# Reordering the score, copy and transpose steps of a first-layer attention pipeline

## The reference

```
xn  = layernorm(x)
q,k,v = Q xn, K xn, V xn              # 16 heads of 64
p   = softmax(causal(q k^T / d_query))
x1  = x + (W (p v) scaled) + ffn(xn)  # ffn: shared unit + 32 experts, top 6, silu(gate) * up
```

## Time and profile before

| | us |
|---|---|
| median of 3 runs (lowest, highest) | 1194.99 (1194.1, 1196.14) |
| the profiled execution | 1194.1 |
| its span | 1192.2 |
| PE busy | 1171.3 (98%) |
| DVE busy | 983.1 (82%) |
| ACT busy | 810.1 (68%) |
| POOL busy | 407.2 (34%) |

### The profile page before, as it was taken

The page is one execution under the profiler, slowest core; times in us unless marked ns, Lnnn a source line. Parts: engine busy times, 40 slices in busy tenths (PEclk is TensorE's granted clock), DMA queues, the critical chain, the costliest instruction groups (busy, mean ns, idle before and its releaser), DMA issues.

```text
span 1192.2 us, 23821 instructions
## 1 busy us (share of the span) xinstructions
PE 1171.3 (98%) x8908; PEld 897.7 (75%) x8908; DVE 983.1 (82%) x1918; ACT 810.1 (68%) x2182; POOL 407.2 (34%) x364
## 2 busy tenths in 40 slices
PE   8999999999999999999999999999999999999998
PEld 6777687767777777677767776777777777767866
DVE  5988588979897989698969886989797878988886
ACT  6885577557755775677567756775577668767775
POOL 1317420640064007300630073006400768526820
PEclk9999999999999999999999999999999999999999
DMA  7004200310041003100410041004100410000000
GB/s 261 2 30 147 88 1 30 125 62 2 30 125 63 1 30 130 58 1 30 134 54 2 30 137 51 2 30 140 47 2 30 151 37 2 10 10 19 1 11 28
DMA packets 44292, 63.93 MB, mean 54 GB/s; under 512 B 8144, under 2 KB 18384, under 8 KB 43920
## 3 DMA queue, kind: packets, MB, share of 16 engines
q1 hardware_dynamic: 44176, 62.39, 16.2%
HBM read 59.48 MB, written 2.88 MB: 52 GB/s over the span
## 4 chain that ended last, share of the span: by engine, by line
PE 82%; DVE 9%; ACT 5%; issue 2%; DMA 1%; SPq 1%; POOL 0%; ACTq 0%; DVEq 0%; POOLq 0%
PE psum L1507 13%; PE psum L1529 12%; PE psum L1454 12%; PE psum L65 10%; PE psum L67 9%; PE psum L66 9%; PE psum L1564 4%; DVE mneg L1146 3%; ACT probs L766 3%; PE psum L1464 2%; PE psum L1756 1%; PE psum L1533 1%; PE psum L1819 1%; PE psum L1406 1%; DVE sg L1196 1%
## 5 line engine op out<-in xcount | busy, mean ns | idle before, releaser
L766 ACT ACTIVATE probs<-psum,mneg 128x256 f32<-128x256 f32 (+3 forms) x528 | 253.0, 495 | 166.5 <-DVE mneg L1146 165.5
L1146 DVE TENSOR_REDUCE mneg<-psum 128x2 f32<-128x1024 f32 (+2 forms) x320 | 245.2, 819 | 46.5 <-PE psum L1464 44.1
L1137 DVE COPY pt<-psum 128x512 f32<-128x512 f32 x320 | 205.7, 682 | 47.4 <-PE psum L1507 45.5
L1507 PE MATMUL psum<-ident,probs 128*128 128x128 f32 x1600 | 210.7, 276 | 3.8 <-DVE pt L1137 1.6
L1507 PEld LDWEIGHTS psum<-ident,probs 128*128 128x128 f32 x1600 | 178.2, 141 | 31.8 <-ACT probs L766 12.2
L573 POOL TENSOR_TENSOR qk_lo<-sg,qk_hi 128x512 fp32r<-128x512 f32 x64 | 92.4, 1450 | 159.0 <-ACT qk_hi L820 159.0
L1529 PE MATMUL psum<-pt,v_all 128*64 128x384 f32 (+5 forms) x1088 | 142.6, 412 | 0.0
L537 POOL TENSOR_TENSOR rstd<-var,mhalf 128x4 f32<-128x4 f32 x7 | 7.1, 1010 | 383.4 <-DVE var L1032 383.4
L1454 PE MATMUL psum<-qk_hi 64*128 64x512 f32 (+7 forms) x640 | 114.2, 353 | 5.4 <-DVE qk_lo L1131 3.6
L1529 PEld LDWEIGHTS psum<-pt,v_all 128*64 128x64 f32 (+1 forms) x1088 | 69.7, 135 | 63.0 <-issue 50.6
L65 PE MATMUL psum<-xt_hi,gu_hi 128*128 128x512 f32 x272 | 111.1, 409 | 0.7 <-DVE sg L1186 0.6
(11 more groups left out here) (276 smaller groups left out, 2506.0 us busy)
## 6 DMA issues: line engine op xcount, KB each, us to landing
crow<-weights SPq DMA_DIRECT2D x256, 128.0 KB, 2.9
rrow<-sums SPq DMA_DIRECT2D x128, 128.0 KB, 3.0
gu_raw<-in_gu SPq DMA_DIRECT2D x1, 2176.0 KB, 11.4
x_all<-in_x SPq DMA_DIRECT2D x8, 256.0 KB, 5.5
out_rows<-x_all SPq DMA_DIRECT2D x7, 256.0 KB, 2.3
down_raw<-in_down SPq DMA_DIRECT2D x1, 1088.0 KB, 13.5
wqkv_raw<-in_wqkv SPq DMA_DIRECT2D x1, 896.0 KB, 6.7
wqkv_raw<-in_wqkv SPq DMA_DIRECT2D x1, 512.0 KB, 4.8
```

The lines of the kernel that those rows point to most:

```text
L766: last = act.activation(probs[:, h * HALF + PROB[t]:h * HALF + PROB[t] + w], bank[score_bank(rnd, c) + h][:, o:o + w], ACT.Exp, bias=mneg[ ...
L1137: dve.tensor_copy(turned_rows(rnd)[:, s % 2, :, 3 - s // 2, :], turn_bank(rnd, s).rearrange("p (j q) -> p j q", q=P)).then_inc(pt_ready, 1)
L1146: last = dve.tensor_reduce(mneg_h[:, :, t], psum[:, b:b + 2, o:o + P * (t + 1)], AX, ALU.max, negate=True)
L1507: last = nc.tensor.transpose(turn_bank(rnd, s)[:, i * P:(i + 1) * P], probs[:, v:v + P], ident[:, :])
```

## The change

- TensorE, in each slot but the last of an item: chunk 2 of round n now comes before chunk 0 of round n+1. The wait for the low part of k of round n+1 stands before chunk 2; the wait for the exponentials stands before chunk 0.
- VectorE, in slots 0 to 5: the copy of T3 now stands before `rest_k`.
- TensorE, slots 6 and 7 and unit 0: `turn_acc` moves from slot 6 to slot 7, behind T0, T1 and T2, which now stand together; it writes bank 6 for all items but the last, and so waits for `copy_y`. T3 and T4 stand alone between the halves of unit 0. The wait on `x1_ready` moves from T0 of slot 7 to the weighted values behind unit 1. VectorE's `add_rows` moves from slot 6 to slot 7.
- ScalarE: the table load with its tiny activation goes from slot 7; a load stands now where the first Silu needs it.

```diff
--- before.py
+++ after.py
@@ -245,7 +245,7 @@
 
         def rows_bank(b):
 
-            return bank[7]
+            return bank[6] if b < B - 1 else bank[7]
 
         WEIGHTS_BANK = bank[6]
 
@@ -858,8 +858,6 @@
                         round_k(n + 2)
                     if p == PAIRS - 2:
                         copy_combt(b)
-                    if p == PAIRS - 1:
-                        load_table(ACT.Silu)
                     take_tile1(n)
                     if b == 0 and p >= PAIRS - len(DOWN_PIECES):
 
@@ -1216,11 +1214,12 @@
                     invert_sums(n)
                     if p < PAIRS - 2:
                         rest_q(n + 2, SCALE0)
-                        rest_k(n + 2)
                     if p < PAIRS - 1:
                         take_turned(n, [3])
-                    if p == PAIRS - 2 and b:
+                    elif b:
                         add_rows(b - 1)
+                    if p < PAIRS - 2:
+                        rest_k(n + 2)
                 n = b * PAIRS + PAIRS - 1
                 for u in range(UNITS):
                     if u == 0:
@@ -1622,14 +1621,15 @@
                     pe.wait_ge(pt_ready, (n - 1) * (TURNS - 1) + 3)
                 score_masks(n, 1, True)
                 score_products(n, 1, n % 2, ROWS0, True).then_inc(scored, 1)
-                if p < PAIRS - 1:
-                    pe.wait_ge(qk_lo_ready, (n + 1) * 2 + 2)
-                    pe.wait_ge(exp_done, exp_count(n, 0))
-                    score_products(n + 1, 0, (n + 1) % 2, ROWS0)
                 if p:
                     pe.wait_ge(pt_ready, n * (TURNS - 1))
                     pe.wait_ge(pt4_ready, n)
+                if p < PAIRS - 1:
+                    pe.wait_ge(qk_lo_ready, (n + 1) * 2 + 2)
                 score_products(n, 2, n % 2, ROWS0)
+                if p < PAIRS - 1:
+                    pe.wait_ge(exp_done, exp_count(n, 0))
+                    score_products(n + 1, 0, (n + 1) % 2, ROWS0)
                 score_masks(n, 2).then_inc(scored, 1)
                 if p < PAIRS - 1:
                     score_masks(n + 1, 0).then_inc(scored, 1)
@@ -1647,11 +1647,6 @@
                     weigh_pair(n - 1)
                 elif b:
                     project_out(b - 1, 3).then_inc(acc_done, 1)
-                if p == PAIRS - 1:
-                    if b:
-                        pe.wait_ge(x1_ready, b)
-                    turn_step0(n, 0)
-                    return
                 for s in range(3):
                     turn_step0(n, s)
                 if p < PAIRS - 2:
@@ -1662,14 +1657,15 @@
                     project_qk(n + 2, [0])
                     pe.wait_ge(pt_ready, n * (TURNS - 1) + 1)
                     project_qk(n + 2, [1])
-                else:
+                elif p == PAIRS - 2:
                     pe.wait_ge(y_ready, n)
                     turn_weights(b)
-                    if b:
-                        pe.wait_ge(pt_ready, n * (TURNS - 1) + 1)
-                        turn_acc(b - 1)
-                turn_step0(n, 3)
-                turn_step0(n, 4)
+                elif b:
+                    pe.wait_ge(y_ready, n)
+                    turn_acc(b - 1)
+                if p < PAIRS - 1:
+                    turn_step0(n, 3)
+                    turn_step0(n, 4)
 
             def first_head(b):
 
@@ -1692,13 +1688,13 @@
             def units(b):
                 n = (b + 1) * PAIRS - 1
                 half_unit(b, 0, 0)
-                turn_step0(n, 1)
-                turn_step0(n, 2)
+                turn_step0(n, 3)
                 half_unit(b, 0, 1).then_inc(gu_done, 1)
-                turn_step0(n, 3)
                 turn_step0(n, 4)
                 pe.wait_ge(pt_ready, n * (TURNS - 1) + 3)
                 project_unit(b, 1)
+                if b:
+                    pe.wait_ge(x1_ready, b)
                 pe.wait_ge(y_ready, n)
                 weigh_pair(n)
                 turn_sums0(b)
```

## The result

The changed kernel takes 1216.24 us (median of 4 runs, 1215.68 to 1217.07) where the kernel before took 1194.55 beside it (4 runs, 1192.04 to 1196.14). The ratio is 1.0184, with a 95% interval of 1.0165 to 1.0203: slower, by 1.7 us more than the forecast of 1214.5, and inside its range. The profiled execution took 1215.57 us, its span 1213.8, so 21.6 us more than before. ScalarE's lines keep their numbers in the changed kernel, VectorE's are 2 less, TensorE's 1 less.

The account below looks back on a forecast made before the run. TensorE was taken as the bound, busy 1171.3 of 1192.2 us. Terms 8.8 - 0.1 + 8.4 + 2.4 = 19.5 us on the profiled 1194.1 gave 1213.6; with the median 0.9 higher, 1214.5 us, range 1202 to 1222.

Parts of the forecast that it names:

- Regular slots: Slots 1 to 5 of eight items: TensorE waits for low k, 0.22 us a slot, 8.8 us in all.
- without any feedback: Regular slots, if a longer slot gave ScalarE and VectorE no earlier start: 0.36 us a slot, the upper bound.
- Slot 6: Without turn_acc seven items save 0.27 but the wait for k adds 0.22: 7.56 us long, -0.1 us in all.
- Slot 7: Up to the weighted values: two late waits and the moved transposes, 1.15 us for seven items, 8.4 us in all.
- the late Silu of 0.15: Item 0, slot 7 term: Silu 0.15 us late since ScalarE also splits weights there.
- The table load: Moved behind T4's copy, ahead of the first Silu: 1.28 us, still hidden with some 0.3 to spare.
- The first units: Units behind the weighted values: VectorE's gates and products about 0.55 later against TensorE; 0.3 us an item, 2.4 in all.
- The first (the wait hides): Rival, regular slots: k is never late, so only slot 7 and the units cost: 1204 us; chance 0.12.
- The second: Rival, not slower: slot 6's 0.27 is saved and turn_acc finds room in slot 7: 1193 us; chance 0.12.
- The clock: Rival: slot 7's two waits lower TensorE's clock in seven items, 12 us more: 1226.5 us; chance 0.05.
- The fourth: Rival, heavier late chain: the table drains or the first units fall behind by 0.8: 1218 to 1222 us; chance 0.09.

Follow-up runs that it names:

- e3: The changed kernel with the wait for low k moved behind chunk 2, ahead of chunk 0, in slots 1 to 6: 1200.79 us, ratio 1.0056.
- e9: The changed kernel with the wait for low k written first of the three waits ahead of chunk 2: 1211.9 us, ratio 1.0152.
- e1: The changed kernel with its slot part undone (chunk order and waits on TensorE, place of the T3 copy on VectorE): 1202.2 us, ratio 1.0061.
- e6: e1 with the accumulator's transposes behind the first half of unit 0 instead of ahead of it: 1199.35 us, ratio 1.0042.
- e7: The kernel before with the table load gone from slot 7 and standing where the first Silu needs it: 1196.75 us, ratio 1.0015.
- e11: The changed kernel with the table load put back behind copy_y in slot 7: 1216.06 us, ratio to before 1.0179.
- e8: The kernel before with ScalarE's high q and k of round 1 ahead of the exponentials of chunk 0 in slot 0: 1192.58 us, ratio 0.999.
- e10: e8 with the copy of the accumulator also ahead of the exponentials of chunk 2 on ScalarE: 1191.18 us, ratio 0.9974.
- e5: The kernel before with TensorE's order alone: chunk 2 ahead of chunk 0, the wait for low k ahead of both: 1208.58 us, ratio 1.0126.
- e2: The kernel before with the slot part of the change alone (TensorE's chunks and waits, VectorE's T3 copy): 1209.84 us, ratio 1.0132.
- e4: The kernel before with VectorE's order alone, the copy of T3 ahead of low k in slots 0 to 5: 1203.56 us, ratio 1.0084.

## Why the prediction was right, and where its sizes were off

**Regular slots: right in mechanism, too small.** The forecast 8.8, measured 12.0. The wait stands where it was said, behind a low k that ends at +1.06 (said: +1.10), and e3 shows that the moved wait is the whole of it. Two sizes were wrong. The start of the waiting matmul was taken as 0.06 behind the low part, from the earlier trace rows, where the late wait is the first of two; it was 0.15, and e9, with 0.05, shows that the rest is the place of the late wait among three (0.09 of a slot). With the late wait written first, slots are 8.53, and the term would be 0.17, a little under the 0.22. And slot 1 was counted like the others: its feedback needs the slot before it to be longer, and slot 0 isn't, so it costs 0.42 (0.34 with the wait first, near the 0.36 that the working had "without any feedback"). 8 x 0.42 + 32 x 0.27 is 12.0.

**Slot 6: right.** 7.60, said 7.56; the 0.04 is the same late wait. In e1, without it, all items have 7.34, so the 0.27 for seven items was really saved.

**Slot 7: right.** 10.17 (said 10.16), 9.20 in item 0 (said 9.36: the late Silu of 0.15 did not come in this stretch, but behind the weighted values, as the next paragraph tells). T1 at +4.51 and the transposes at +5.91 are the two waits, and item 0, which has T1's alone, lost 0.19 of the 0.20 given to it. e6 takes the second away and gets 0.53 back. That the remaining 0.46 are the four transposes is by difference (1.15 - 0.19 - 0.49); no run took them out.

**The table load: right in items 1 to 7, wrong in item 0.** It is 1.28 and Silu begins 0.01 behind it. In items 1 to 7 neither e7 nor e11 changes slot 7 or unit 2. The first gate, which unit 2 needs, is the first half of the two drawn from 337.88 for 1.28, so it ends at about 338.5, over 0.4 us ahead of unit 2 at 339.00, where 0.4 was worked out. For item 0 the working gave the late Silu 0.15. That much came at unit 2 (2.51 behind the weighted values, 2.37 before), but unit 4 then waits another 1.17 for its gate. The chain of Silu, gate 0, gate 1, product and normalisations was worked out for item 2, and item 0, with more in ScalarE's list, was priced by its first gate alone. The 1.38 to drain that the Trainium skill (ScalarE: Activation LUTs, "What ACT_TABLE_LOAD costs") adds isn't in these traces.

**The first units: said 2.4, measured 1.1, and the nearness is luck.** In items 1 to 7 the gate of unit 2 now ends at 342.48 and unit 4 starts at 342.58, so of the 0.57 of room 0.47 is used, near the 0.55 of the working, and then almost nothing is lost: unit 4 is 5.95 behind the weighted values (5.94 before), and the next pair 0.08 later. That is 0.5 us in all, where I had put 0.3 an item. The rest of the 1.1 was in no term: 1.4 net in item 0 from the moved load, 1.6 the other way from before's low clock, and in the other items changes of -0.3 to +0.6, the larger ones by the waits near 26.2 us behind the weighted values, whose choice of item stays open.

**The rivals.** The first (the wait hides) fell with 8.62. The second named the saving of slot 6 rightly, but copy_y stayed at +5.85. The clock stayed at 1.00 in slot 7 and in the regular slots with their new waits. The fourth fell in items 1 to 7 with unit 4 on time; in item 0 the late chain is real, but costs 0.9 to 1.5 us and not 4 to 8. The misses, 3.2 too little in the slots and 1.3 too much in the units, partly cancel: the total was better than its terms.

## What to carry to other kernels

Before a wait is moved forward, list everything that the new place asks for, and look which of it the releasing engine makes last: here VectorE makes three things in a row, and in both orders that were run the third was late at +0.98. Keeping the wait at its point of use took the loss away (e3). Where several waits stand before one group, write the one that comes last first. And when a wait is taken away and the slot gets no shorter, read the next slot: a second engine that works without a gap from one into the other (ScalarE in e8 and e10) hands the same time back. And price a moved step in each kind of item: what hid in seven items showed in the one where ScalarE had more to do.

## What the runs showed of the hardware

- After a late wait TensorE's matmul started 0.05 to 0.06 us behind its releaser where that wait is the first of its group in the source (e9, e5), and 0.15 behind it where two others stand before it (the change). Over 48 slots that was about 4.4 us.
- The same wait of about 1.95 us in slot 0 of item 0 has three outcomes, which are mixes of the 2.4 GHz level with the lower one of 1.2 GHz. In seven profiled executions the granted clock stays at 1.00 and the slot takes 9.5 us. In two (before and e6) it is 0.83 over 20 to 30 us, and the slot takes 9.8. In two (e5 and e7) it is 0.74 and 0.77 there and 0.91 and 0.89 in the next 10 us, and the slot takes 11.9 and 12.0. In e8 and e10, where the wait is 1.04 us, the clock is 1.00 and the slot takes 7.92. The stretch of the change with this wait:

```profile
20.00:30.00 10.00, 6.90 (x67) 5.33 (x67) 7.07 (x12) 7.58 (x24) 0.00 (x0) 1.00 0.66 160
```

  So the earlier trace rows are no property of the kernel before. The runs fit with that: those of before beside e10 lie between 1192.41 and 1197.26 (23 runs), and those of e10 between 1190.49 and 1192.43 (12 runs). In e7's profiled execution this slot is most of the excess over before, so the size of the table load is read from item 0's first units and not from the spans; whether the edit makes the slower outcome more frequent stays open.
- A shorter wait, of 0.64 to 0.78 us in item 0's later units, has two outcomes. Seven profiled executions have it. In three (before, e2, e11) the granted clock is 0.83 over 115 to 125 us and item 0's last stretch takes 55.4 to 55.5 us; in four (e4, e5, e8, e10) it is 1.00 and the stretch takes 53.9 to 54.0.
